# Two attentions in one kernel: the penalty of every first tile of the top-k stage moves to GpSimd with a new order of work, and the second attention runs its pairs through the heads and divides at the end

## The reference

```python
# layer 0
q, k, v = heads(conv1x1(x, Wq, bq)), ...                       # (B, 8, N, 32)
scores = einsum('bhnd,bhmd->bhnm', q, k) * 32 ** -0.5
kth = top_k(scores, 64)[0][..., -1:]
attn = softmax(where(scores >= kth, scores, finfo.min))        # only the 64 largest of each row
o = conv1x1(einsum('bhnm,bhmd->bhnd', attn, v), Wo, bo) + x
h1 = relu(batchnorm(conv1x1(o, W1, b1), g1, be1))              # 256 -> 1024
x = batchnorm(conv1x1(h1, W2, b2), g2, be2) + o                # 1024 -> 256
# layer 1
xn = x / max(norm over channels, 1e-12) * g * 16
q, k, v = split(einsum('oc,bchw->bohw', w_qkv, xn))
attn = softmax(einsum('bhdi,bhdj->bhij', q * 32 ** -0.5, k))   # full softmax
out = einsum('oc,bchw->bohw', w_out, attn @ v) + b_out + x
```

## Time and profile before

| | us |
|---|---|
| three runs, median (lowest to highest) | 5586.61 (5582.31 to 5589.42) |
| profiled execution | 5584.55 |
| its span, first to last instruction | 5582.5 |
| PE busy, 32459 instructions | 4367.2 (78%) |
| DVE busy, 25684 | 4406.7 (79%) |
| ACT busy, 6084 | 4164.0 (75%) |
| POOL busy, 362 | 1502.2 (27%) |

### The profile page before, as it was taken

The page is one execution under the profiler, slowest core; times in us unless marked ns, Lnnn a source line. Parts: engine busy times, 40 slices in busy tenths (PEclk is TensorE's granted clock), DMA queues, the critical chain, the costliest instruction groups (busy, mean ns, idle before and its releaser), DMA issues. The chain is left out here.

```text
span 5582.5 us, 114219 instructions
## 1 busy us (share of the span) xinstructions
PE 4367.2 (78%) x32459; PEld 2805.0 (50%) x32459; DVE 4406.7 (79%) x25684; ACT 4164.0 (75%) x6084; POOL 1502.2 (27%) x362
## 2 busy tenths in 40 slices
PE   7575677766777477677777678988999999999998
PEld 4443445544544244445544454445655655655655
DVE  4999999989999999999999993224777777777775
ACT  2786799988988589889998893433666766666664
POOL 0443444444544244444554440010000000000000
PEclk8777677777777677777777779989999999999999
DMA  5000000000000000000000001014010010010012
GB/s 198 6 17 14 7 17 17 9 14 17 16 8 16 5 16 17 15 7 17 17 7 17 16 16 44 8 40 158 22 29 21 22 30 21 21 30 21 22 30 86
DMA packets 79607, 154.88 MB, mean 28 GB/s; under 512 B 8120, under 2 KB 49464, under 8 KB 73528
## 3 DMA queue, kind: packets, MB, share of 16 engines
q1 hardware_dynamic: 78904, 146.72, 9.3%
HBM read 99.50 MB, written 47.19 MB: 26 GB/s over the span
## 5 line engine op out<-in xcount | busy, mean ns | idle before, releaser
L539 POOL TENSOR_TENSOR a_probs<-a_scores,a_probs 128x2304 f32<-128x2304 f32 x288 | 1460.3, 5090 | 1778.2 <-ACT a_probs L462 1778.2
L557 DVE MAX8 a_top<-a_scores 128x8 f32<-128x36 f32 x18432 | 1831.2, 180 | 46.4 <-ACT a_scores L446 45.7
L373 PE MATMUL a_ps_t<-ident,a_probs 128*128 128x128 f32 x5184 | 976.2, 326 | 702.5 <-ACT a_probs_t L457 570.8
L373 PEld LDWEIGHTS a_ps_t<-ident,a_probs 128*128 128x128 f32 x5184 | 675.5, 164 | 989.4 <-ACT a_probs_t L457 707.5
L1110 PE MATMUL b_ps_t<-ident,b_soft 128*128 128x128 f32 x5184 | 794.3, 286 | 97.9 <-ACT b_soft_t L1183 69.6
L462 ACT ACTIVATE a_probs<-a_scores,a_steep_kth 128x2304 f32<-128x2304 f32 x290 | 641.2, 2211 | 294.7 <-DVE a_minus_max L667 294.7
L1195 DVE TENSOR_SCALAR_CACHE_REDUCE b_soft<-b_ps_s 128x2304 f32<-128x2304 f32 x290 | 741.7, 2558 | 86.9 <-PE b_ps_s L1097 67.3
L1183 ACT ACTIVATE b_soft_t<-b_ps_t 128x512 f32<-128x512 f32 (+1 forms) x864 | 438.0, 525 | 473.2 <-PE b_ps_t L1110 472.5
L1110 PEld LDWEIGHTS b_ps_t<-ident,b_soft 128*128 128x128 f32 x5184 | 557.6, 142 | 450.8 <-issue 304.2
L457 ACT ACTIVATE a_probs_t<-a_ps_t 128x512 f32<-128x512 f32 (+1 forms) x1440 | 726.8, 545 | 20.7 <-PE a_ps_t L373 7.2
L1168 ACT ACTIVATE b_soft<-b_soft,b_minus_max 128x2304 f32<-128x2304 f32 x289 | 642.1, 2222 | 30.2 <-issue 16.8
(11 more groups left out here) (127 smaller groups left out, 4279.6 us busy)
## 6 DMA issues: line engine op xcount, KB each, us to landing
a_k_stack<-k_parts SPq DMA_DIRECT2D x72, 288.0 KB, 6.0
b_k_stack<-k_parts SPq DMA_DIRECT2D x72, 288.0 KB, 6.1
a_q_ring<-q_parts SPq DMA_DIRECT2D x294, 64.0 KB
b_q_ring<-q_parts SPq DMA_DIRECT2D x294, 64.0 KB
k_parts<-p_high SPq DMA_DIRECT2D x36, 256.0 KB, 2.1
k_parts<-p_rest SPq DMA_DIRECT2D x36, 256.0 KB, 2.2
q_parts<-p_high SPq DMA_DIRECT2D x36, 256.0 KB, 2.0
q_parts<-p_rest SPq DMA_DIRECT2D x36, 256.0 KB, 2.0
```

Of the source, the lines that this page charges most:

```text
L373: last = pe.transpose(ps_t[(NTG * s + g) % 2][:, P * m:P * m + P], probs[s % 2][:, P * (m0 + m):P * (m0 + m) + P], cst["ident"][:, :])
L539: pool.tensor_tensor(probs[u][:, :], scores_all[:, 2 * (p % 2) + u, :], probs[u][:, :], ALU.subtract).then_inc(masked_ready, 1)
L557: last = dve.max(top8[s // 2 % 2][:, s % 2, c, :], scores_all[:, s % 4, CHUNK * c:CHUNK * c + CHUNK])
```

## The change

In `attention_top`:
- The penalty of the first tile of each pair is made by GpSimd (`tensor_scalar` with is_lt and a factor, 128x2304, from a new `kept_kth`), behind which GpSimd's own subtraction follows. ScalarE makes only the second tile's penalty.
- On VectorE `select` stands ahead of the first MAX8 of a pair, its last part is split off as `pick` behind the 24th MAX8, and `hand_on` moves behind the 48th. `hand_on` writes one more small tile, `kept_kth`.
- TensorE, ScalarE and GpSimd have new orders; those of TensorE and ScalarE now run pair steps through the heads, with the first and last written out.

In `attention_full` the pair steps run through the heads (a loop of 7 with the rest written out), scores are issued in two pieces between transposes, the products with values stand in two blocks of three and two groups, the quadrants are turned by two transposes and added by a `tensor_reduce` on VectorE, and there is no reciprocal or multiplication with it. The sums are kept for all heads. In `output` the division is done as in `project_out`: a reciprocal, two divisions ahead of the loop, and seven in it.

The third division (chunk 2) stands behind the two additions of chunk 0. The diff, cut to its core (the conditions of the first and last pair steps are left out):

```diff
 # attention_top, VectorE
                 dve.tensor_scalar(steep_kth[parity][:, :], kth[:, :], STEEP, None, ALU.mult)
+                dve.tensor_scalar(kept_kth[parity][:, :], kth[:, :], 1.0, None, ALU.mult)
                 dve.tensor_scalar(minus_max[parity][:, :], extremes[:, :, 0], -SCALE, None,
                                   ALU.mult).then_inc(kth_ready, 1)
...
+                found = select(pair - 1, top8[(p - 1) % 2]) if before else None
                 def between(c):
-                    if c == 7 and before:
-                        select(pair - 1, top8[(p - 1) % 2])
-                    if c == 19 and before:
+                    if c == 23 and before:
+                        pick(found)
+                    if c == 47 and before:
                         hand_on(pair - 1, (p - 1) % 2)
 # attention_top, GpSimd
-                    for u in range(2):
-                        pool.wait_ge(penalty_ready, tile + u + 1)
-                        pool.tensor_tensor(probs[u][:, :], scores_all[:, 2 * (p % 2) + u, :], probs[u][:, :],
-                                           ALU.subtract).then_inc(masked_ready, 1)
+            def subtract(u, pair, parity, first=False):
+                if u == 0:
+                    if not first:
+                        wait_alone(pool, turned, pair * (2 * NTG) - NTG)
+                    wait_alone(pool, kth_ready, pair + 1)
+                    pool.tensor_scalar(probs[0][:, :], scores_all[:, 2 * parity, :], kept_kth[parity][:, 0:1], -LOWEST,
+                                       ALU.is_lt, ALU.mult).then_inc(first_penalty, 1)
+                    pool.wait_ge(first_penalty, pair + 1)
+                else:
+                    pool.wait_ge(penalty_ready, pair + 1)
+                pool.tensor_tensor(probs[u][:, :], scores_all[:, 2 * parity + u, :], probs[u][:, :],
+                                   ALU.subtract).then_inc(masked_ready, 1)
 # attention_top, ScalarE: one pair step
+                keep_scores(p + 2, 0, h)
+                exponentials(p, 0, h)
+                keep_turned(p, 0, 0, h)
+                keep_parts(pair - 1)
+                keep_turned(p, 0, 1, h)
+                keep_turned(p, 0, 2, h)
+                keep_any(pair + 1)
+                keep_scores(p + 2, 1, h)
+                keep_turned(p, 0, 3, h)
+                finish(p - 1, h)
+                keep_turned(p, 0, 4, h)
+                exponentials(p, 1, h)
+                guess_place(p + 2, 0, h)
+                for g in range(4):
+                    keep_turned(p, 1, g, h)
+                guess_place(p + 2, 1, h)
+                keep_turned(p, 1, 4, h)
+                penalty(p + 1, 1, h)
 # attention_full, TensorE
+            def pair_step(p, h, before=2, ahead=True):
+                turn(s, 0, tile)
+                turn_parts(pair - 2)
+                score(s + 2, h, tile + 2, range(0, 2))
+                turn(s, 1, tile)
+                score(s + 2, h, tile + 2, range(2, 5))
+                turn(s, 2, tile)
+                turn(s, 3, tile)
+                for g in range(3):
+                    weigh(p - 1, g, pair - 1, h)
+                turn(s, 4, tile)
+                turn(s + 1, 0, tile + 1)
+                score(s + 3, h, tile + 3, range(0, 1))
+                turn(s + 1, 1, tile + 1)
+                score(s + 3, h, tile + 3, range(1, 5))
+                turn(s + 1, 2, tile + 1)
+                turn(s + 1, 3, tile + 1)
+                for g in range(3, NTG):
+                    weigh(p - 1, g, pair - 1, h)
+                turn(s + 1, 4, tile + 1)
-            with pe.Fori(0, HEADS) as h:
-                for p in range(HEAD_PAIRS):
+            with pe.Fori(0, HEADS - 1) as h:
+                for p in range(2, HEAD_PAIRS + 2):
+                    pair_step(p, h)
...
+                    last = pe.transpose(ps_o[:, PAIR + P * u:PAIR + P * u + P], parts[:, P * u:P * u + P],
+                                        cst["ident"][:, :])
 # attention_full, VectorE
-                    last = dve.tensor_scalar(o_all[:, s, cols(h * D, D)], ps_o[:, PAIR + D * u:PAIR + D * u + D],
-                                             one_by_sum[s % 6][:, 0:1], None, ALU.mult)
+                dve.tensor_reduce(o_all[:, 2 * p:2 * p + 2, cols((h + ahead) * D, D)],
+                                  ps_o[:, PAIR:2 * PAIR].rearrange("p (u q d) -> p u d q", u=2, q=4),
+                                  AX.X, ALU.add).then_inc(o_ready, 1)
 # output
             def turn(c):
+                pe.wait_ge(divided, c + 1)
...
+            dve.reciprocal(one_by_sum[:, :, :], sums[:, :, :]).then_inc(inverse_ready, 1)
+            dve.wait_ge(inverse_ready, 1)
+            divide(0)
+            divide(1)
...
+                if c + 2 < NCH:
+                    divide(c + 2)
```

435 lines of the change are left out of this document (238 added, 197 removed).

## The result

| | kernel before | kernel after |
|---|---|---|
| median, us | 5585.26 (5582.31 to 5589.42) | 6470.76 (6463.28 to 6474.01) |
| ratio, 95% interval | | 1.158 (1.156 to 1.160) |
| span of the profiled execution, us | 5582.5 | 6461.5 |
| top-k stage, first to last `steep_kth`, us | 3208.9 | 4364.8 |
| one pair there, median of 143 intervals, us | 20.70 | 28.81 |

A forecast was written before the change was run, and what follows sets the result against it. VectorE was taken to bound the top-k stage, TensorE the second attention and output. Terms +16 - 167 - 27 + 21.5 = -156.5 from 5584.55 gave 5428, with the median's offset 5430 us; range 5350 to 5535.

The forecast's parts named there:

- The penalty's price: Top-k stage, GpSimd: the new first-tile penalty, which had no row, taken as 3.1 us between bounds 2.7 and 10.8.
- one constant of 0.45: Top-k stage, GpSimd: fixed cost that, with the copy's rate, explained both rows behind the 3.1 us penalty.
- the limit at 4.0 us: Top-k stage: a longer penalty pushes GpSimd's second subtraction onto `select`, 5.3 us a pair, time 6190; rival's chance 0.15.
- L648 or L650: Top-k stage, VectorE: sign of a wrong forecast, these rows taking 5 us or having a gap ahead in each pair.
- The layout of the pair: Top-k stage: new order laid out from `steep_kth`, `select` fitting between GpSimd's subtractions; 20.5 us a pair, -0.06 each, -9 in all.
- The end of a head: Top-k stage: VectorE's branch delays `select` until GpSimd's subtraction ends, +4.5 us at each of 7 ends, +31.
- End of the stage: Top-k stage's last step no longer computes scores, penalties and guesses of absent tiles: some 6 us shorter.
- ScalarE's relief: Top-k stage: the 2.22 us penalty that ScalarE loses buys almost nothing, since VectorE stays the bound.
- Second attention: TensorE's pair there falls from 11.01 to 9.85 us, 1.16 gained 144 times: -167 us.
- My sum of work: Second attention, TensorE's pair: work of 9.08 us, plus 0.7 to 0.97 for 12 changes between kinds of work.
- Heads' ends: Second attention: each of 7 ends costs 4 us instead of 7.8, draining and refilling gone, branch kept: -27 us.
- Output: Output stage: +21.5 us, from +7.9 waiting for the third division, +11.9 for six later turns and +1.7 for slower work.

The follow-up runs named there:

- experiment 4: Kernel before with a piece put ahead: seven GpSimd forms alone, then VectorE forms alone and beside three of them; 5835.3 us in a single execution.
- experiment 7: Changed kernel with GpSimd's penalty replaced by a plain copy, comparison left out, so output not that of the reference; median 5299.1 us, 0.949 of the kernel before.
- Experiment 6: Changed kernel's new order with both penalties on ScalarE, the first ahead of the second tile's exponentials; 5659.4 us, 1.013 of the kernel before.
- Experiment 10: Old top-k stage with the changed second attention and output, all nine output divisions moved ahead of the wait for x1; 5287.9 us, ratio 0.9465.

## Why the prediction was wrong, point by point

- **The penalty's price: the step that failed.** "I take 3.1", between 2.7 and 10.8. It is 8.04 us (experiment 4: 6.1 with one operation, 1.9 for the second). I chose the end near the copy because one constant of 0.45 explained both rows. But the two rows were of different operations, and the one of the same operation (`TENSOR_SCALAR`, with one operation an element) pointed to the other end. It should have outweighed the copy, and between ends so far apart neither was near enough to choose by. The Trainium skill ("GPSIMD Engine Reference", section "Elementwise — side-by-side cycle accounting") has the cost per element the same for one and two operations. The Trainium skill ("GPSIMD Engine Reference", section "Engine selection") also calls one input "roughly line-rate". Here a second operation cost 1.9 us, and a `TENSOR_SCALAR` with one operation three times a copy (6.15 against 2.13 us), so the measurement decides against both.
- **What follows from the price.** The prediction put the limit at 4.0 us and said what lies beyond: "the penalty takes over 4.0 us and pushes it there", 5.3 us a pair, 6190 us, chance 0.15. The mechanism was named rightly; 8.1 us a pair came instead of 5.3, since not one but two subtractions in a row fall on `select`: the penalty ends at 2023.4, and ScalarE's own penalty, which ends at 2026.45, is early for the second. The rows that stop are L636 and L639, and not the L648 or L650 that I had named as the sign. (144 x 5.3 is 763 and not 757, which changes nothing.) With two bounds so far apart on either side of a limit of 4.0, 0.15 was too little.
- **The layout of the pair**: right (experiment 7: 20.47 us for the forecast 20.45), though the forecast counted from one pair of 20.51 us where the median was 20.70, so the ordinary pair gained 0.23 us and not 0.06. The end of a head was forecast at +4.5 us each: with the copy, the pairs there took 26.6 us against 23.3 before, +3.3, at six of the seven. In the kernel as timed there was no such extra; the ordinary pairs were shut out already.
- **End of the stage**: -6 forecast, -0.7 measured, with the copy -1.0 (528.7 us to the first `shift` against 529.7). Wrong, and small.
- **ScalarE's relief buys almost nothing**: right. With a cheap penalty, first to last `steep_kth` gained 8 us, where the forecast for this stretch was a loss of 22 (-9 for the pairs, +31 for the ends of heads). Experiment 6 adds what I had not said: the new order would cost 350 us without that relief.
- **Second attention**: 9.12 us for the forecast 9.85, a gain of 270 instead of 167. By the starts of TensorE's rows the transposes fell from 5.36 us, 0.47 of them idle, to 4.09, the value products from 2.84 to 2.42, the quadrants from 0.37 to 0.16; scores stayed at 2.45. My sum of work was 9.08, and the 0.7 to 0.97 that I added for changes between kinds of work is the term that was mis-sized: the pair took 9.11. That isn't because a change costs nothing. In the kernel before, four transposes between two blocks of value products take 0.59 us (below) with no idle time shown; in the changed one, four between two pieces of scores take 0.35 (5207.71 to 5208.06). A block with one group of products takes 0.57 us and one with three 1.43 (5209.78 to the next transposes at 5211.22), so a group costs 0.43 and each block 0.14 on top. The old pair has five blocks and the new one two. By pricing a single block at 0.57 I had part of this in the sum already and then added it again. That the 9.08 itself fits is in part luck: the transposes came out 0.24 over my 3.85, the products and the turned parts 0.21 under theirs. Heads' ends: (1645.4 - 144.5 x 10.99) / 7 = 8.2 before and (1338.6 - 143.5 x 9.12) / 7 = 4.3 now; forecast 7.8 and 4.
- **Output**: forecast +21.5, of which 7.9 for the third division (7.2 measured) and 1.98 for each later turn (1.98). By the marks it came to some +18 (29.4 less the 11 that belong to the fifth term). Experiment 10 took 21.8 away again.

TensorE before, two rows of the second attention beside the earlier trace rows:

```profile
4202.23 0.66 PE L1110 MATMUL b_ps_t<-ident,b_soft 128*128 128x128 f32 x4
4202.82 0.64 PE L1128 MATMUL b_ps_o<-b_soft_t,b_v 128*32 128x256 f32 x8
```

With a first step of 2.1 us the sum would have been 2.5% off: 5430 against the 5299 of experiment 7. Of those 131 us, 103 lie in the second attention's pairs and 25 in the top-k stage (+16 forecast, -9 measured).

## What to carry to other kernels

Before work goes to GpSimd, look for a row of the same form there, not of the same size, and if there is none, measure that form alone. Then lay its instructions over VectorE's small plain ones (two inputs from SBUF, or a scalar form without accumulator): each of these that starts while a GpSimd instruction runs stands until that one is through, so the cost is what is left of GpSimd's instruction, not the length of VectorE's. Where the overlap can't be avoided, cut GpSimd's work into pieces, and take the work off an engine only if that engine is the bound.
